# Macaron block with gated linear attention on 8 cores: the normalised head output transposed by DMA with gamma and beta applied by ScalarE, and one set of input tiles requested later

## The reference

```python
x = x + 0.5 * ffn(layernorm(x), W)          # first half step
x = x + attn(layernorm(x), Wq, Wk, Wv, Wg, Wo, gamma, beta)
x = x + 0.5 * ffn(layernorm(x), W)          # second half step
# ffn: rows of x to 8-bit steps, W to -1/0/1, y = x_q @ w_q.T * alpha * beta_row
# attn: q, k, v and g = log_sigmoid(x @ Wg.T), 16 heads of 128;
#   S = S * exp(g_t) + k_t v_t ;  y_t = q_t S          (along the tokens)
#   o = (layernorm(y) * gamma + beta) @ Wo.T
```

## Time and profile before

| | us |
|---|---|
| median of 3 runs | 3469.9 (3467.58 to 3722.14) |
| profiled execution, its time | 3467.16 |
| its span, slowest core (core 7) | 3465.6 |
| span of the other cores | 3440.9 (core 5) to 3464.2 (core 6) |
| mean granted TensorE clock | 0.990 to 0.992 of full speed |
| PE busy on core 7 | 3321.8 (96%) |
| DVE / ACT busy on core 7 | 2018.9 (58%) / 744.6 (21%) |

### The profile page before, as it was taken

The page is one execution under the profiler, slowest core; times in us unless marked ns, Lnnn a source line. Parts: engine busy times, 40 slices in busy tenths (PEclk is TensorE's granted clock), DMA queues, the critical chain, the costliest instruction groups (busy, mean ns, idle before and its releaser), DMA issues.

```text
span 3465.6 us, 49427 instructions; the slowest of 8 cores (3440.9 to 3465.6 us)
## 1 busy us (share of the span) xinstructions
PE 3321.8 (96%) x18210; PEld 1611.7 (47%) x18210; DVE 2018.9 (58%) x3783; ACT 744.6 (21%) x1297; POOL 48.3 (1%) x94
## 2 busy tenths in 40 slices
PE   1789998999999999999999999999999999999999
PEld 0334453445544454445544455444554455444544
DVE  5626767156672666637664476826667366635663
ACT  5312321023200221113211232002320032112210
POOL 0000000000000000000000000000000000000000
PEclk9899999999999999999999999999999999999999
DMA  7899979787566546665466655666556654553453
GB/s 221 193 225 204 219 179 231 202 199 195 177 194 200 170 159 183 191 198 170 150 188 204 177 169 171 182 200 172 176 168 197 202 157 161 163 170 145 153 176 134
DMA packets 227642, 634.68 MB, mean 183 GB/s; under 512 B 165856, under 2 KB 165888, under 8 KB 189520
## 3 DMA queue, kind: packets, MB, share of 16 engines
q1 hardware_dynamic: 215104, 553.68, 49.3%
q0 software_dynamic: 12304, 77.85, 14.6%
HBM read 585.35 MB, written 83.89 MB: 193 GB/s over the span
## 4 chain that ended last, share of the span: by engine, by line
PE 87%; DMA 9%; DVE 1%; issue 1%; another core or an unknown queue 1%; SPq 0%; ACT 0%; DVEq 0%; POOLq 0%; ACTq 0%; POOL 0%
PE pj L511 47%; PE pj L597 35%; DMA ring<-wh 2%; DMA s_v<-first 1%; DMA ring<-wv 1%; DMA s_h<-ring 1%; DMA fw<-fw 1%; PE pT L488 1%; DMA ring<-wo 1%; PE pP L571 1%; PE pY L581 1%; PE pT L546 1%; PE pA L554 1%; PE pY L584 1%
## 5 line engine op out<-in xcount | busy, mean ns | idle before, releaser
L511 PE MATMUL pj<-ring,xT 128*128 128x512 bf16 x8000 | 1755.4, 380 | 31.5 <-DVE bnA L722 12.4
L597 PE MATMUL pj<-xT,ring 128*128 128x512 bf16 x6144 | 1369.3, 380 | 28.2 <-DMA ring<-wh 23.6
L511 PEld LDWEIGHTS pj<-ring,xT 128*128 128x128 f16 (+1 forms) x8000 | 779.1, 98 | 955.0 <-issue 45.1
L597 PEld LDWEIGHTS pj<-xT,ring 128*128 128x128 bf16 x6144 | 590.4, 98 | 711.5 <-issue 40.8
L765 DVE TENSOR_TENSOR_SCAN Cs<-rest_s,lsg 128x512 f32<-128x512 bf16 x128 | 156.6, 1223 | 301.8 <-ACT lsg L1049 300.6
L962 DVE SCALAR_TENSOR_TENSOR ost<-pj,coC,res 128x512 f32<-128x512 f32 x112 | 84.1, 751 | 405.5 <-PE pj L511 405.5
L1046 ACT ACTIVATE lsg<-pj 128x512 f32<-128x512 f32 x128 | 76.4, 597 | 736.4 <-PE pj L597 729.6
L759 DVE SCALAR_TENSOR_TENSOR res<-pj,coA,res 128x512 bf16<-128x512 f32 x128 | 95.7, 748 | 174.4 <-PE pj L511 174.4
L804 DVE TENSOR_TENSOR qt<-pj,E 128x512 bf16<-128x512 f32 x128 | 88.4, 691 | 133.1 <-PE pj L597 133.1
L1039 ACT CAST vy<-pY 128x512 bf16<-128x512 f32 x128 | 75.0, 586 | 369.5 <-PE pY L584 349.4
L1083 ACT CAST vy<-pj 128x512 bf16<-128x512 f32 x128 | 74.9, 585 | 366.9 <-PE pj L511 366.9
(11 more groups left out here) (121 smaller groups left out, 2187.1 us busy)
## 6 DMA issues: line engine op xcount, KB each, us to landing
ring<-s_h SPq DMA_DIRECT2D x108, 1536.0 KB, 8.2
ring<-s_f SPq DMA_DIRECT2D x60, 2048.0 KB, 9.3
ring<-s_v SPq DMA_DIRECT2D x28, 2048.0 KB, 9.9
ring<-s_o SPq DMA_DIRECT2D x28, 2048.0 KB, 9.8
out<-ost SPq DMA_DIRECT2D x128, 256.0 KB, 4.3
ring<-wh POOLq DMA_DIRECT2D x20, 1536.0 KB, 21.7
s_h<-ring SPq DMA_DIRECT2D x16, 1536.0 KB, 20.2
fw<-fw SPq DMA_DIRECT2D x16, 1024.0 KB, 35.9
```

What stands on the lines that cost most here:

```text
L511: return e.matmul(bank(phase, k)[:], xt[:, ic * SLAB + t * 128:ic * SLAB + (t + 1) * 128], buf(n)[:, ic * 512:(ic + 1) * 512], start=ic == ...
L597: mm = e.matmul(bank(phase, 3 * h + j)[:], buf(n)[:, ic * 384 + j * 128:ic * 384 + (j + 1) * 128], xt[:, ic * SLAB:(ic + 1) * SLAB], start ...
```

## The change

Three edits. (1) Y crosses for slabs 1 to 6; for these PE's 8 turns go (`turns_of_y` gives none), SP issues the four transposing DMAs, two after the load of P4's block 0 and two after the load of its block 1. (2) For the same slabs ACT applies gamma and beta in place in `xT`: `scaled(g, t)` waits for the crossing of tile t and runs 16 ACTIVATEs of 128x128, one for each block; all four tiles stand at k = 6 of ACT's tail, behind `rstd("Y", g)`. PE's first four groups of P4 wait for ACT's last ACTIVATE of their tile. (3) The extra x tiles of slab 2 wait for the last group of P4(0) as well.

```diff
         def crossed(kind, g):
-            return (kind in "AL" and g >= 2) or (kind == "C" and g < NSL - 1)
+            return (kind in "AL" and g >= 2) or (kind == "C" and g < NSL - 1) or (kind == "Y" and 0 < g < NSL - 1)
...
         def turns_of_y(g, k):
+            if crossed("Y", g):
+                return ()
...
                 (kind, g), b = done
+                if kind == "P1" and g > 0 and crossed("Y", g - 1) and 1 <= b <= 2:
+                    cross("Y", g - 1, 2 * b - 2)
+                    cross("Y", g - 1, 2 * b - 1)
...
                     e.wait_ge(*TD.of("Y", g - 2, 3, 3))
+                    if g == 2:
+                        e.wait_ge(*TD.of("fat", ("P4", 0), 15))
                     for t in range(TPS):
                         e.dma_start(out=xe(t), in_=xrows[g * TPS + t]).then_inc(*XE[t].up(g, by=16))
...
                         if k < TPS and ic == 0:
-                            e.wait_ge(*XT[t].of(kind, g))
+                            e.wait_ge(*(SD.of("gb", g, t) if kind == "Y" else XT[t].of(kind, g)))
...
                 for i in turns_of_y(g, k):
                     turned("Y", g, i)
+                if k == 6 and crossed("Y", g):
+                    for t in range(TPS):
+                        scaled(g, t)
+
+            def scaled(g, t):
+                dst = xTof(g)
+                e.wait_ge(*XT[t].of("Y", g))
+                for ic in range(NB):
+                    cs = slice(ic * SLAB + t * 128, ic * SLAB + (t + 1) * 128)
+                    e.activation(dst[:, cs], dst[:, cs], ACTF.Identity, bias=bet[:, ic:ic + 1],
+                                 scale=gam[:, ic:ic + 1]).then_inc(*SD.up("gb", g, t))
```

## The result

| | before | changed |
|---|---|---|
| median us | 3469.9 | 3497.2 |
| ratio | 1 | 1.0076, 95% interval 1.0042 to 1.0110 |
| profiled execution's span, slowest core | 3465.6 | 3494.4 (core 1) |

In a second session the unaltered changed kernel gave 1.0072 (1.0052 to 1.0091). So it is slower by 0.7%, some 26 us, well inside the 2% of a verdict, but clear of no change. The forecast was 3490, +20.

A forecast was written before the change was run, and what follows sets the result against it. PE, busy 96%, was taken to bound the kernel. 24.5 (slabs 1 to 5) + 0.5 (slab 6) + 7 (clock) - 12 (later x tiles) = +20 on the profiled 3467.2, 3487; the median 2.7 higher, so 3490, range 3475 to 3505.

The forecast's parts named there:

- ACT's 64 ACTIVATEs: ACT's scaling in each crossed slab: 0.37 us per ACTIVATE, 5.9 us a tile, 23.7 us for four tiles.
- When ACT can start: Before P4, slab 2: tile 0 lands at 1336.3, its block 0 load issued at 1318.24 being slowed by x tiles.
- The rest of the chain: After ACT's scaling: rstd of L, DVE normalising L, then P4's first bank emptied, free 4.35 us after F.
- F: Time when ACT finishes its 64 ACTIVATEs: 1360.0 in slab 2; nothing is lost if below 1351.5.
- Slab 6: P4's start without extra x tiles behind it: bank 0 free at 1360.0 in slab 2's time, +0.5 us.
- The clock: PE at lower clock after a new 7 us gap before P4's group 3: 1.4 us in each of five slabs, 7 us.
- The later x tiles: Before V(1): weights come sooner without slab 2's x tiles, 10.6 us of the 12.4 us gap plus 1.4 clock, -12 us.
- A: Rival at P4's start: ACT is in time and the 21.6 us stay, 3436 us; chance 0.10.
- B: Rival: crossings do not wait for x tiles, tile 0 at 1330 in all slabs, about even, 3461 us; chance 0.14.
- C: Rival: crossings lose against x tiles, or held SP makes tile 2 late (after 1348.4), 3516 us; chance 0.13.
- D: Rival: the skill's TensorE transpose price holds (219 ns each, 84 us) and ACT is hidden, 3374 us; chance 0.01.
- E: Rival before V(1): later x tiles do nothing, Wo's cast and write-back hold the weights, 3502 us; chance 0.10.

The follow-up runs named there:

- no_scale: The changed kernel without ACT's 384 scaling ACTIVATEs, so gamma and beta are missing in slabs 1 to 6: ratio 0.9923, 3433.2 us.
- cross_first: The changed kernel with every slab's extra x tiles after P4's last group and all four Y crossings issued before P4's block 0 load: ratio 0.9892.
- rstd_between: The changed kernel with rstd of L moved on ACT to between the scaling of tiles 1 and 2, same work: ratio 1.0012, 3466.6 us.
- x_later_all: The changed kernel with the extra x tiles of every slab, not only slab 2, asked for after P4's last group: ratio 0.9992, 3460.8 us.
- x_later_only: The kernel before with the third edit alone, slab 2's extra x tiles waiting for P4(0)'s last group: ratio 0.9962, 3453.1 us.
- changed_again: The changed kernel unaltered, run again in a later session as a control: ratio 1.0072, 3485.7 us.

## Why the prediction was right

- **What leaves PE**: 3.6 us a slab. no_scale and cross_first show 410.1 - 406.5 = 3.6. Right.
- **ACT's 64 ACTIVATEs**: I took 0.37 us apart, 23.7 in all. Measured (24.88 - 0.48) / 63 = 0.387 and 24.9, 1.2 more. At 256 columns they are (7.97 - 0.59) / 15 = 0.492 apart, so a column costs 0.82 ns, about the 0.85 that I took; the part paid once per instruction was low by 0.02. The estimate from the Trainium skill (ScalarE: Activation LUTs, What ACT_TABLE_LOAD costs), 0.386, was the better one: the trace agrees with it.
- **When ACT can start**: 18.1 us after block 0's load by my count, 16.9 measured. The load landed after 13.7 us for the 15.9 that I took over, and the crossing 3.1 behind it for 2.2. By luck this 1.2 us cancels the 1.2 above: ACT ended 41.8 us after the load, as predicted.
- **The rest of the chain**: rstd, normalise, first bank, F + 4.35. Measured 1360.64 - 1356.40 = 4.24. Group 3 came 5.0 us later than before; predicted 4.9. The mechanism, ACT's row holding rstd of L and through it DVE and bank 0, is what rstd_between shows.
- **Slab 6**: +0.5 predicted, 0.0 measured for the stretch. But I gave its 3.4 us of idleness no clock, and the slab's part to the end of the program came out 2.8 us longer (510.7 from block 0's load to the end, 508.0 before).
- **The clock**: "5 x 1.4 = 7 us". It is 2.0 a slab, 10 us, and some 2.8 in slab 6. This term was mis-sized by 6 us, the largest miss. (Its source was also read 0.1 us low: 141 matmuls at 0.216 are 30.5 us, so core 3 lost 1.5.) That a wait of 3 us can cost as much clock as one of 7 was not in the prediction.
- **The later x tiles**: -12 predicted, -12 to -13 measured.
- **Sum**: 25 + 10 + 2.8 - 12 = +26, against 26 by the ratio and 20 by the forecast. The mechanism was right; the clock's 6 us are the whole of the miss.
- **SP's loads**: block 1's load left 1.8 us later in its phase than before, not 4: 17.0 us after block 0's, where it was 15.2 before (1333.4, not "about 1332") and PE would have allowed 13.8.
- **The rivals**: A needed 0.24 us an ACTIVATE. B, tile 0 early in all slabs, is x_later_all, where it is a fact. B gave it 9 us under the kernel before; measured are 3 by the ratio. Its half microsecond a slab lacks the clock behind the wait of 3.3 us that even then is left, and slabs are 1.5 to 2 us longer. C's point was near: SP was held, and tile 2 landed at 1332.62 + 11.3 = 1343.9, just when ACT was done with tile 1, as in the forecast; any later and it would have counted. C's sentence on passing 2% has a wrong sum: 69 us less the forecast's 20 are 49, some 10 us more in each of five slabs, not 14. D's price was absent. E was refuted by x_later_only.

## What to carry to other kernels

When work moves from the bounding engine to an idle one, look at what stands behind it in that engine's queue. ACT was 21% busy, yet 64 small instructions in one spot held a 0.5 us `rstd`, through it DVE, and through DVE a PSUM bank; moving the rstd gave back 4.4 of the 10.6 us, and getting the work's input 12 us sooner gave back all of it. At 128 and 256 columns count small instructions by their number, not by their columns, and put a short transfer that somebody is waiting for ahead of a long one that has slack.

## What the runs showed of the hardware

- A gap of PE can cost more than its length, and by how much does not follow its length. In the changed kernel and changed_again, slabs 1 to 5 on all eight cores, P4's group 2 took the usual 3.61 us behind the waits of 0.6 to 1.9 us. Behind the waits of 2.0 to 3.1 us it took up to 5.30 in some slabs and 3.61 in others, as on core 3 of the changed kernel in slabs 1 and 2:

```profile
917.80 5.30 PE L519 MATMUL pj<-ring,xT 128*128 128x512 bf16 x16 [2.35 <-ACT xT L1096]
...
1336.31 3.61 PE L519 MATMUL pj<-ring,xT 128*128 128x512 bf16 x16 [2.99 <-ACT xT L1096]
```

- Behind longer waits the clock stayed at 0.50 for a while, which loses half of that while: for 5.8 us behind 3.39 us (slab 6), 4.1 behind 6.89 us (slab 2), and 2.9 behind the 7.00 us on core 3 of the kernel before.
- Matmuls whose result nobody reads keep the clock at 1.00 over such a gap, and were worth 2.0 us a slab.
- A crossing of 512 KB lands after 4.3 us alone, 10.1 beside x tiles and 16.4 behind a 2 MB load with x tiles in flight. The queue that issues it is held meanwhile: SP spent 14.3 us on the last of these.
